# First layer's selective scan: softplus as one ScalarE function, one y image added to in all four directions, straight writes to PSUM

## The chip, the cores and the metric

The kernel runs on one core of one Trainium2 chip. A core has five engines with a queue each: TensorE (PE, matrix products, into PSUM), VectorE (DVE), ScalarE (ACT, functions from tables), GpSimd (POOL, no access to PSUM) and SyncE (SP, which here issues DMA transfers). They meet through semaphores alone. The metric is the device time of one launch in microseconds. A median of several runs is compared with a median; the profile is one further execution.

## What is computed

Two layers of a vision network, each a state-space (Mamba-like) mixer and a small quantised feed-forward net, on x of 4 x 48 x 64 x 64. The change touches the first mixer, after its convolution and projections:

```python
# z: 4 images x 96 channels x 64 x 64, K = 4 directions, one state per channel
x0 = z.reshape(B, D_INNER, L)                        # along rows
x1 = swapaxes(z, 2, 3).reshape(B, D_INNER, L)        # along columns
xs = stack([x0, x1, flip(x0), flip(x1)], axis=1)
x_dbl = einsum('bkdl,ked->bkel', xs, x_proj_weight)  # gives dts_r (3), Bs (1), Cs (1)
delta = softplus(einsum('bkrl,kdr->bkdl', dts_r, dt_projs_weight) + bias)
dA  = exp(delta * A)                                 # A = -exp(A_logs)
dBu = delta * Bs * xs
h[t] = dA[t] * h[t-1] + dBu[t]                       # scan over L = 4096 positions
y = h * Cs + Ds * xs
ym = y0 + unswap(y1) + flip(y2) + unswap(flip(y3))   # the four directions, in one image
```

Then come layer norm, an output product, and the rest of the network, which the change leaves alone.

## The kernel before

Five phases follow each other with a barrier between them: `front0_phase`, `scan0_phase`, `back0_phase`, `mid1_phase`, `back1_phase`. The change lies in `scan0_phase` (L821 to L1111).

**Tiling.** The 4 images x 32 channels of a group fill the 128 partitions, J = 3 groups (index j) cover the 96 channels. A direction's 4096 positions are walked in NTC = 4 pieces of TC = 1024. `steps` (L845) lists n = 16 steps for a group: directions 1 and 3 (down the columns, forward and back), then 0 and 2 (along the rows, forward and back), so 8 column steps and then 8 row steps; 48 steps in all. A half of a piece is CH = 512 positions, one bank of PSUM. i counts steps through all groups.

**A step, engine by engine.** TensorE makes dt before softplus in PSUM (`dt_of`, L925 to L936, tile q_dt, two halves, one buffer), and spreads B and C over the partitions half by half (`spread`, L938 to L945, tiles q_b and q_c, one buffer each). In a column step the moving operand is read in runs of 8 elements and the result is written with a stride through `by_rows`, so that PSUM holds the order of the scan. ScalarE computes |dt|, exp(-|dt|) and ln(1 + ..) (L991, L993, L995, tile b_l), VectorE adds max(dt, 0) to it (`delta_of`, L1014, tile b_dl): that is softplus. ScalarE makes the decay dA = exp(delta A) into PSUM (L983, tile b_qa). GpSimd multiplies delta by z (L1097, tile b_u; z is seen with a stride in a column step). VectorE multiplies that by B half by half (`drive`, L1020), scans (L1031, tile b_h) and multiplies by C (`times_c`).

**The sum over directions.** There are two images in SBUF, `yrow` and `ycol`. Direction 1 is written to `ycol` by `times_c` itself (L1044). The other three go through b_g (L1048) and are added by GpSimd (L1111) to `ycol` or `yrow`. ScalarE starts `yrow` as z times the sum of D (L1003). Before the last pieces GpSimd merges `ycol`, read with a stride, into `yrow` (`merge`, L1086, four times a group). SyncE stores the finished pieces.

**What sets the order.** It is written out by hand, in each engine's function. VectorE's turn for step i: first drive, first C product of step i-1, delta of i+1, second drive, second C product, scan. GpSimd: product of step i, then (from step 4 of a group) merge, then the add of step i-2. Buffers b_l, b_dl, b_u, b_h, b_g and b_qa are double.

## Time and profile before

| | us |
|---|---|
| median of 3 runs | 1626.08 |
| lowest, highest | 1622.43, 1626.56 |
| the profiled execution | 1625.65 |
| its span, first to last instruction | 1623.8 |
| first product of the scan on VectorE to the end of its last scan | 221.88 to 515.38 |

The page's groups name line, engine, output and inputs, shapes and count; then busy time and mean duration; then the idle time of the engine before such instructions and what ended it. The timeline gives start and duration; a bracket behind an instruction tells how long its engine idled and what released it, and its absence means that the engine was busy until then. Neighbouring instructions of an engine overlap by about 0.1 us, so cadence is read from starts.

### The profile page before, as it was taken

How to read it: one execution, taken by the hardware profiler on the slowest of the kernel's cores; microseconds unless marked ns; L12 is line 12 of the kernel's file. 1: busy time of each engine (PE TensorE's matmuls, PEld its weight loads, DVE VectorE, ACT ScalarE, POOL GpSimd, SP SyncE). 2: the span in 40 equal slices, each digit the busy share in tenths (PEclk: the TensorE clock that was granted, in tenths of full speed). 3: DMA queues.
4: the chain of work that ended last, by engine and by line, in shares of the span. 5: the costliest groups of instructions: out<-in, count | busy, mean ns of one | idle time of the engine just before them, and what ended most of it. 6: DMA issues, size and time to landing. Idle time of an engine off the chain costs nothing. (4 is left out here: it accounts for less than half of the span.)

```text
span 1623.8 us, 14529 instructions
## 1 busy us (share of the span) xinstructions
PE 1286.5 (79%) x3822; PEld 436.9 (27%) x3822; DVE 1271.7 (78%) x1274; ACT 1154.7 (71%) x1691; POOL 898.3 (55%) x451
## 2 busy tenths in 40 slices
PE   4999757585763577768789988998989889776995
PEld 2444201010110355532122222222222222111663
DVE  1665659999996477730999999999999999894775
ACT  2677358687773477748898898889898988641564
POOL 2400037969788333313987787888787888750000
PEclk8999955555555799978788889888897898555998
DMA  5344480200101233225877787777787877634572
GB/s 153 106 137 124 109 183 0 84 20 1 52 1 63 68 97 98 83 56 149 193 180 171 183 190 175 175 174 182 167 183 181 187 172 162 132 71 105 130 175 67
DMA packets 136429, 200.54 MB, mean 123 GB/s; under 512 B 26739, under 2 KB 68770, under 8 KB 135564
## 3 DMA queue, kind: packets, MB, share of 16 engines
q1 hardware_dynamic: 133740, 196.15, 49.5%
q10 hardware_dynamic: 2160, 2.61, 0.6%
q0 software_dynamic: 448, 0.85, 0.2%
q8 instruction: 32, 0.52, 0.1%
q14 instruction: 49, 0.40, 0.1%
HBM read 145.93 MB, written 53.63 MB: 123 GB/s over the span
## 5 line engine op out<-in xcount | busy, mean ns | idle before, releaser
L1375 POOL TENSOR_TENSOR m_ub<-m_dlb,m_bt 128x1536 f32<-128x1536 f32 x128 | 440.2, 3441 | 144.1 <-DVE m_h L1729 136.8
L1729 DVE TENSOR_TENSOR_SCAN m_h<-m_qa,m_state,m_ub 128x512 f32<-128x512 f32 x384 | 463.8, 1262 | 53.4 <-POOL m_ub L1375 51.9
L1691 ACT ACTIVATE m_qa<-m_dlb,k_a 128x512 f32<-128x512 f32 x384 | 254.8, 684 | 107.9 <-DVE m_h L1729 102.0
L1097 POOL TENSOR_TENSOR b_u<-b_dl,b_z 128x1024 f32<-128x1024 f32 x48 | 125.2, 2608 | 212.0 <-DVE b_dl L1014 211.4
L1740 DVE TENSOR_TENSOR m_g<-m_h,m_qc 128x1536 f32<-128x1536 f32 x128 | 221.7, 1732 | 14.3 <-issue 7.7
L1558 PE MATMUL m_qc<-m_bcr,k_selc 32*128 32x512 f32 x256 | 167.5, 738 | 81.8 <-DVE m_g L1740 81.6
L1575 PE MATMUL m_qy<-m_g,k_seld 128*32 128x512 f32 x768 | 169.5, 743 | 0.0
L944 PE MATMUL b_qb<-b_bc,k_pack_sel 96*128 96x512 bf16 x96 | 81.6, 850 | 73.6 <-DVE b_u L1020 71.0
L1499 PE MATMUL m_qf<-m_cva,k_conv 113*96 113x504 f32 (+1 forms) x192 | 124.4, 799 | 5.0 <-PEq L1131 5.0
L1558 PEld LDWEIGHTS m_qc<-m_bcr,k_selc 32*128 32x128 f32 x256 | 42.9, 209 | 205.7 <-issue 188.7
L983 ACT ACTIVATE b_qa<-b_dl,b_a 128x1024 f32<-128x1024 f32 x48 | 53.7, 1118 | 62.2 <-DVE b_dl L1014 62.2
L935 PE MATMUL b_qdt<-b_dt,b_wdt 75*128 75x512 bf16 x96 | 69.9, 852 | 34.0 <-DVE b_dl L1014 19.0
L526 PE MATMUL n_q<-a_cv,k_conv 113*96 113x504 f32 (+1 forms) x192 | 91.0, 611 | 2.6 <-DVE a_acc L545 2.4
L944 PE MATMUL b_qc<-b_bc,k_pack_sel 96*128 96x512 bf16 x96 | 84.1, 876 | 7.0 <-DVE b_g L1048 7.0
L1031 DVE TENSOR_TENSOR_SCAN b_h<-b_qa,b_h,b_u 128x1024 f32<-128x1024 f32 x36 | 84.5, 2347 | 0.0
L1020 DVE TENSOR_TENSOR b_u<-b_u,b_qb 128x512 f32<-128x512 f32 x96 | 65.0, 677 | 14.6 <-POOL b_u L1097 8.3
L1014 DVE SCALAR_TENSOR_TENSOR b_dl<-b_qdt,b_l 128x1024 f32<-128x1024 f32 x48 | 58.7, 1223 | 16.3 <-ACT b_l L995 16.1
L1499 PEld LDWEIGHTS m_qf<-m_cva,k_conv 113*96 113x96 f32 x192 | 41.1, 232 | 104.2 <-issue 104.2
L545 DVE SCALAR_TENSOR_TENSOR a_acc<-a_low,k_pack_d,n_q 96x512 f32<-96x512 f32 x32 | 23.7, 742 | 54.9 <-PE n_q L526 41.1
L991 ACT ACTIVATE b_l<-b_qdt 128x512 f32<-128x512 f32 x96 | 54.2, 590 | 13.9 <-PE b_qdt L935 12.7
L1657 ACT ACTIVATE m_tp<-m_u,k_pack_d 96x512 f32<-96x512 f32 x96 | 62.3, 712 | 0.8
L362 ACT ACTIVATE f_h<-g_q 96x1024 f16<-96x1024 f32 x32 | 32.6, 1020 | 39.0 <-PE g_q L356 39.0
(181 smaller groups left out, 2478.9 us busy)
## 6 DMA issues: line engine op xcount, KB each, us to landing
m_dlb<-scratch_dldu SPq DMA_DIRECT2D x128, 384.0 KB, 9.6
m_bt<-scratch_brow SPq DMA_DIRECT2D x128, 256.0 KB, 5.8
scratch_dldu<-m_dldu SPq DMA_DIRECT2D x32, 384.0 KB, 5.0
scratch_z<-a_z SPq DMA_DIRECT2D x24, 256.0 KB, 6.0
b_z<-scratch_z SPq DMA_DIRECT2D x3, 2048.0 KB, 11.4
scratch_y<-b_yrow SPq DMA_DIRECT2D x12, 512.0 KB, 2.6
c_y<-scratch_y SPq DMA_DIRECT2D x16, 384.0 KB, 3.4
scratch_gate<-m_gt SPq DMA_DIRECT2D x32, 192.0 KB, 4.8
```

What stands on the lines that cost most here:

```text
L526: last = self.nc.tensor.matmul(out[:, :, o], self.pairs[:, tap, :], src[:, :, i], start=(tap == 1), stop=(tap == 2))
L935: nc.tensor.matmul(by_rows(q_dt[:, v * CH:v * CH + CH], col), wdt[:, j, k, :], seen_rows(dtx[k][:], col, piece, v), start=True, stop=True) ...
L944: nc.tensor.matmul(by_rows(q[:], col), G["selbc0"][:, row + k, :], seen_rows(bcx[:], col, piece, v), start=True, stop=True).then_inc(ready, 1)
L1031: nc.vector.tensor_tensor_scan(h[s][:, way], q_a[s][:, way], u[s][:, way], carried, ALU.mult, ALU.add).then_inc(scanned, 1)
L1097: nc.gpsimd.tensor_tensor(by_column(u[s][:], col), by_column(dl[s][:], col), seen(z[j % 2][:], col, piece), ALU.mult).then_inc(u_ready, 1)
L1375: nc.gpsimd.tensor_tensor(ub[k % 3][:], dlb[u % 2][:, J:2 * J, :], bcast(bt[u % 2][:, n, :], J), ALU.mult).then_inc(ub_ready, 1)
L1499: nc.tensor.matmul(out[:, :, o], G["conv1"][:, tap, :], src[:, :, i], start=(tap == 1), stop=False)
L1558: nc.tensor.matmul(q_c[:], G["selc"][DI:P, 4 * n:4 * n + 4, :], bcr[u % 4][DI:P, :], start=True, stop=True).then_inc(c_mm, 1)
L1575: last = nc.tensor.matmul(q_y[32 * j:32 * j + 32, :], G["seld"][:], g[k % 2][:, j, :], start=(n == 0), stop=(n == 3))
L1691: nc.scalar.activation(q_a[:, j, :], dlb[u % 2][:, j, :], ACT.Exp, scale=G["a1"][:, j, n:n + 1]).then_inc(da, 1)
L1729: nc.vector.tensor_tensor_scan(h[k % 3][:, j, :], q_a[:, j, :], ub[k % 3][:, j, :], state[:, k % NS, j:j + 1], ALU.mult, ALU.add).then_inc ...
L1740: nc.vector.tensor_tensor(g[k % 2][:], h[k % 3][:], bcast(q_c[:], J), ALU.mult).then_inc(read, 1)
```

## The change

- Softplus is ScalarE's own function and reads q_dt: two halves a step, straight into b_dl. |dt|, Exp, Ln and VectorE's sum fall away. The function lies in another table than Exp, so steps are taken in pairs: load the Exp table, two decays (and perhaps a piece of y), load the softplus table, four softplus halves. b_dl has DL = 4 buffers.
- TensorE writes PSUM in the order in which it reads (`in_rows`). The readers of q_dt, q_b and q_c turn the order in a column step by their own pattern (`from_rows`, a step of 8 words).
- There is one y image, in the order of the rows, with two buffers b_y over the groups. Every direction goes through b_g, and GpSimd adds each piece to it; in a column step it reads and writes y with a stride. The merge falls away. y is begun for group 0 at the start and for the next groups in the last 8 steps of the one before.
- Direction 2 comes before direction 0, so that the last pass stores its pieces from 0 to 3.
- The loops run on over all 48 steps without a turn per group. TensorE's dt products for steps i+2 and i+3 stand in odd iterations, the first between the two halves of B and C.

The core of the diff:

```diff
-        yrow, ycol = (m.sb(f"b_{n}", [P, T]) for n in ("yrow", "ycol"))
+        y = [m.sb(f"b_y{r}", [P, T]) for r in range(2)]
...
+        dl = [m.sb(f"b_dl{s}", [P, TC]) for s in range(DL)]
...
-        order = [(1, 1, 0), (3, 1, 1), (0, 0, 0), (2, 0, 1)]
+        order = [(1, 1, 0), (3, 1, 1), (2, 0, 1), (0, 0, 0)]
...
-        def by_rows(ap, col):
+        def in_rows(ap, col):
-            return ap.rearrange("p (w h) -> p h w", h=H) if col else ap
+            return ap.rearrange("p (h w) -> p h w", h=H) if col else ap
+        def from_rows(ap, col):
+            return ap.rearrange("p (h w) -> p w h", h=H) if col else ap
...
# TensorE
-                pe.wait_ge(delta, freed(i, 1))
                 for v in range(TC // CH):
-                    nc.tensor.matmul(by_rows(q_dt[:, v * CH:v * CH + CH], col), wdt[:, j, k, :],
+                    pe.wait_ge(delta, half(i - 1, v))
+                    nc.tensor.matmul(in_rows(q_dt[:, v * CH:v * CH + CH], col), wdt[:, j, k, :],
...
+            for i in range(last + 1):
+                for o in range(2):
+                    if i < last:
+                        spread(i // n, i % n, o, q_b, 0, driven, b_mm)
+                    if i > 0:
+                        spread((i - 1) // n, (i - 1) % n, o, q_c, K4, read, c_mm)
+                    if o == 0 and i % 2 == 1:
+                        ahead(i, 2)
+                if i == 0:
+                    ahead(i, 2)
+                if i % 2 == 1:
+                    ahead(i, 3)
# ScalarE
-                            nc.scalar.activation(sp_l[s][:, part], q_dt[:, part], ACT.Abs).then_inc(absd, 1)
-                        nc.scalar.activation(sp_l[s][:], sp_l[s][:], ACT.Exp, scale=-1.0).then_inc(expd, 1)
-                        nc.scalar.activation(sp_l[s][:], sp_l[s][:], ACT.Ln, bias=G["eps"][:, 2:3]).then_inc(lnd, 1)
+            def delta_of(i):
+                s, col = i % DL, steps[i % n][1]
+                act.wait_ge(da_ready, freed(i, DL))
+                act.wait_ge(u_ready, freed(i, DL))
+                for v in range(TC // CH):
+                    part = slice(v * CH, v * CH + CH)
+                    act.wait_ge(dt_mm, half(i, v))
+                    nc.scalar.activation(by_column(dl[s][:, part], col), from_rows(q_dt[:, part], col), ACT.Softplus).then_inc(delta, 1)
...
+            for i in range(0, last, 2):
+                act.preload_act_table_set(LOG_EXP_SET)
+                decay(i)
+                decay(i + 1)
+                if i == 0:
+                    for c in range(NTC):
+                        begin_y(0, c)
+                if i // n + 1 < J and i % n >= n - 2 * NTC:
+                    begin_y(i // n + 1, (i % n - n + 2 * NTC) // 2)
+                if i + 2 < last:
+                    act.preload_act_table_set(SOFTPLUS_SET)
+                    delta_of(i + 2)
+                    delta_of(i + 3)
# VectorE
-                nc.vector.scalar_tensor_tensor(dl[s][:], q_dt[:], 0.0, sp_l[s][:], ALU.max, ALU.add).then_inc(delta, 1)
...
-                nc.vector.tensor_tensor(u[s][:, part], u[s][:, part], q_b[:], ALU.mult).then_inc(driven, 1)
+                half_u = by_column(u[s][:, part], col)
+                nc.vector.tensor_tensor(half_u, half_u, from_rows(q_b[:], col), ALU.mult).then_inc(driven, 1)
...
+                dve.wait_ge(added, freed(i))
+                nc.vector.tensor_tensor(by_column(g[s][:, part], col), by_column(h[s][:, part], col), from_rows(q_c[:], col),
+                                        ALU.mult).then_inc(read, 1)
# GpSimd
-                nc.gpsimd.tensor_tensor(part, part, ycol[:].rearrange("p (w h) -> p h w", w=W)[:, rows, :],
-                                        ALU.add).then_inc(merged, 1)
...
-                    nc.gpsimd.tensor_tensor(y, y, g[s][:], ALU.add).then_inc(added, 1)
+                    pool.wait_ge(added, done(i - 3))
+                    part = seen(y[j % 2][:], col, piece)
+                    nc.gpsimd.tensor_tensor(part, part, by_column(g[i % 2][:], col), ALU.add).then_inc(added, 1)
```

How the change moves the instructions is seen best in a row step in the middle of a pass. On VectorE, one row step before (b_u, b_qb: the drives; b_g, b_h, b_qc: the C products; the last line is the scan):

```order
L1020 TENSOR_TENSOR b_u1<-b_u1,b_qb 128x512
L1048 TENSOR_TENSOR b_g0<-b_h0,b_qc 128x512
L1014 SCALAR_TENSOR_TENSOR b_dl0<-b_qdt,b_l0 128x1024
L1020 TENSOR_TENSOR b_u1<-b_u1,b_qb 128x512
L1048 TENSOR_TENSOR b_g0<-b_h0,b_qc 128x512
L1031 SCALAR_TENSOR_TENSOR b_h1<-b_qa1,b_h0,b_u1 128x1024
```

And the same step in the changed kernel:

```order
L1021 TENSOR_TENSOR b_u1<-b_u1,b_qb 128x512
L1043 TENSOR_TENSOR b_g0<-b_h0,b_qc 128x512
L1021 TENSOR_TENSOR b_u1<-b_u1,b_qb 128x512
L1043 TENSOR_TENSOR b_g0<-b_h0,b_qc 128x512
L1032 SCALAR_TENSOR_TENSOR b_h1<-b_qa1,b_h0,b_u1 128x1024
```

The instruction that makes b_dl is gone, and only a C product is left between the two drives, each of which reads b_qb.

On ScalarE, one step of the second slice of a group before (b_l: the parts of softplus; b_qa: the decay; b_yrow: y begun):

```order
L983 ACTIVATE b_qa<-b_dl,b_a 128x1024
L991 ACTIVATE b_l<-b_qdt 128x512 x2
L993 ACTIVATE b_l<-b_l 128x1024
L995 ACTIVATE b_l<-b_l,k_pack_norm 128x1024
L1003 ACTIVATE b_yrow<-b_z,b_dsum 128x1024
```

And a pair of steps in the changed kernel:

```order
L999 ACT_TABLE_LOAD
L981 ACTIVATE b_qa<-b_dl,b_a 128x1024 x2
L990 ACTIVATE b_y<-b_z,b_dsum 128x1024
L1008 ACT_TABLE_LOAD
L974 ACTIVATE b_dl<-b_qdt 128x512 x4
```

Two steps' decays, then two steps' softplus, with a table load ahead of each kind.

On GpSimd, two row steps with a merge before (b_u: the product with z; the line that reads b_ycol: the merge):

```order
L1097 TENSOR_TENSOR b_u<-b_dl,b_z 128x1024
L1086 TENSOR_TENSOR b_yrow<-b_yrow,b_ycol 128x1024
L1111 TENSOR_TENSOR b_yrow<-b_yrow,b_g 128x1024
L1097 TENSOR_TENSOR b_u<-b_dl,b_z 128x1024
L1111 TENSOR_TENSOR b_yrow<-b_yrow,b_g 128x1024
```

And the column steps of the changed kernel, where the add has a form of 16 columns by 64 positions:

```order
L1074 TENSOR_TENSOR b_u<-b_dl,b_z 128x1024
L1085 TENSOR_TENSOR b_y<-b_y,b_g 128x16x64
L1074 TENSOR_TENSOR b_u<-b_dl,b_z 128x1024
L1085 TENSOR_TENSOR b_y<-b_y,b_g 128x16x64
L1074 TENSOR_TENSOR b_u<-b_dl,b_z 128x1024
```

Products and adds alternate in every step from the third on, and nothing stands between them.

## Rows read from the trace of the kernel before

**Rows 1.** The page: TensorE's busy us and share; granted clock in 40 slices.

```profile
PE 1286.5 (79%) x3822; PEld 436.9 (27%) x3822; DVE 1271.7 (78%) x1274; ACT 1154.7 (71%) x1691; POOL 898.3 (55%) x451
...
PEclk8999955555555799978788889888897898555998
```

**Rows 2.** Windows: length, busy us (count) by engine, granted clock, DMA share, GB/s.

```profile
250.00:283.00 33.00, 23.79 (x35) 3.28 (x33) 32.43 (x34) 26.70 (x30) 26.04 (x12) 0.50 0.00 0
450.00:483.00 33.00, 23.60 (x36) 3.55 (x36) 32.43 (x35) 26.50 (x31) 27.13 (x11) 0.50 0.00 1
```

**Rows 3.** Groups, 200 to 525 us: shapes, count, busy us, mean ns, idle before.

```profile
L1097 POOL TENSOR_TENSOR b_u<-b_dl,b_z 128x1024 f32<-128x1024 f32 x48 | 125.2, 2608 | 212.0 <-DVE b_dl L1014 211.4
...
L1014 DVE SCALAR_TENSOR_TENSOR b_dl<-b_qdt,b_l 128x1024 f32<-128x1024 f32 x48 | 58.7, 1223 | 16.3 <-ACT b_l L995 16.1
L1111 POOL TENSOR_TENSOR b_yrow<-b_yrow,b_g 128x1024 f32<-128x1024 f32 x24 | 56.5, 2353 | 1.1 <-POOL b_yrow L1111 0.2
...
L991 ACT ACTIVATE b_l<-b_qdt 128x512 f32<-128x512 f32 x96 | 54.2, 590 | 13.9 <-PE b_qdt L935 12.7
L983 ACT ACTIVATE b_qa<-b_dl,b_a 128x1024 f32<-128x1024 f32 x48 | 53.7, 1118 | 62.2 <-DVE b_dl L1014 62.2
...
L1086 POOL TENSOR_TENSOR b_yrow<-b_yrow,b_ycol 128x1024 f32<-128x1024 f32 x12 | 34.4, 2867 | 0.5 <-DVE b_g L1048 0.5
```

**Rows 4.** Timeline, row steps: start us, us, instruction [idle before <-releaser].

```profile
475.35 0.69 DVE L1020 TENSOR_TENSOR b_u<-b_u,b_qb 128x512 f32<-128x512 f32 x1
475.94 0.69 DVE L1048 TENSOR_TENSOR b_g<-b_h,b_qc 128x512 f32<-128x512 f32 x1
476.54 2.35 DVE L1031 TENSOR_TENSOR_SCAN b_h<-b_qa,b_h,b_u 128x1024 f32<-128x1024 f32 x1
...
477.83 2.87 POOL L1086 TENSOR_TENSOR b_yrow<-b_yrow,b_ycol 128x1024 f32<-128x1024 f32 x1
478.80 0.68 DVE L1020 TENSOR_TENSOR b_u<-b_u,b_qb 128x512 f32<-128x512 f32 x1
...
480.78 2.35 POOL L1111 TENSOR_TENSOR b_yrow<-b_yrow,b_g 128x1024 f32<-128x1024 f32 x1
...
483.10 2.35 POOL L1097 TENSOR_TENSOR b_u<-b_dl,b_z 128x1024 f32<-128x1024 f32 x1
...
485.47 0.69 DVE L1020 TENSOR_TENSOR b_u<-b_u,b_qb 128x512 f32<-128x512 f32 x1 [0.81 <-POOL b_u L1097]
```

**Rows 5.** Timeline, two column steps of the first slice.

```profile
254.33 1.12 ACT L983 ACTIVATE b_qa<-b_dl,b_a 128x1024 f32<-128x1024 f32 x1 [0.25 <-DVE b_dl L1014]
254.35 1.89 PE L935 MATMUL b_qdt<-b_dt,b_wdt 75*128 75x512 bf16 x2 [0.25 <-DVE b_dl L1014]
254.38 2.86 POOL L1097 TENSOR_TENSOR b_u<-b_dl,b_z 128x1024 f32<-128x1024 f32 x1 [3.25 <-DVE b_dl L1014]
...
258.38 1.03 PE L944 MATMUL b_qb<-b_bc,k_pack_sel 96*128 96x512 bf16 x1 [0.43 <-DVE b_u L1020]
...
260.44 1.12 ACT L983 ACTIVATE b_qa<-b_dl,b_a 128x1024 f32<-128x1024 f32 x1 [0.26 <-DVE b_dl L1014]
...
260.55 1.01 PE L935 MATMUL b_qdt<-b_dt,b_wdt 75*128 75x512 bf16 x2 [0.28 <-DVE b_dl L1014]
```

**Rows 6.** Timeline, the last steps, on VectorE, TensorE and GpSimd.

```profile
510.36 0.69 DVE L1020 TENSOR_TENSOR b_u<-b_u,b_qb 128x512 f32<-128x512 f32 x1 [0.81 <-POOL b_u L1097]
...
511.11 0.61 PE L944 MATMUL b_qb<-b_bc,k_pack_sel 96*128 96x512 bf16 x1 [3.15 <-DVE b_u L1020]
...
511.82 0.69 DVE L1020 TENSOR_TENSOR b_u<-b_u,b_qb 128x512 f32<-128x512 f32 x1 [0.18 <-PE b_qb L944]
...
513.03 2.35 DVE L1031 TENSOR_TENSOR_SCAN b_h<-b_qa,b_h,b_u 128x1024 f32<-128x1024 f32 x1
...
516.12 2.34 POOL L1111 TENSOR_TENSOR b_yrow<-b_yrow,b_g 128x1024 f32<-128x1024 f32 x1
...
516.85 0.69 DVE L1048 TENSOR_TENSOR b_g<-b_h,b_qc 128x512 f32<-128x512 f32 x1 [0.76 <-PE b_qc L944]
...
518.63 2.34 POOL L1111 TENSOR_TENSOR b_yrow<-b_yrow,b_g 128x1024 f32<-128x1024 f32 x1 [0.17 <-POOL b_yrow L1111]
```

**Rows 7.** Timeline, ScalarE in a later phase: a table load and softplus.

```profile
901.74 1.28 ACT L1674 ACT_TABLE_LOAD   x1
903.03 0.59 ACT L1678 ACTIVATE m_dldu<-m_qg 96x512 f32<-96x512 f32 x1
903.65 1.28 ACT L1679 ACT_TABLE_LOAD   x1
```

**Rows 8.** Timeline, the first steps of the scan.

```profile
220.73 1.03 PE L944 MATMUL b_qb<-b_bc,k_pack_sel 96*128 96x512 bf16 x1 [2.47 <-DMA b_bc<-scratch_bc]
221.88 0.69 DVE L1020 TENSOR_TENSOR b_u<-b_u,b_qb 128x512 f32<-128x512 f32 x1 [5.57 <-PE b_qb L944]
```

179 lines of the change are left out of this document (63 added, 116 removed).

## The prediction

> **What bounds the kernel now.** The change touches one phase, the first layer's scan, so I read that phase alone. The page shows a TensorE that runs at about half clock there: slices 5 to 12 of the clock line are 5s, and the windows say 0.50, the 1.2 GHz level [rows 1, 2]. The windows then name the engine: in 33 us VectorE is busy 32.43 us, ScalarE 26.6, GpSimd 26 to 27, TensorE under 24 [rows 2]. The scan's first product on VectorE starts at 221.88 [rows 8], its last scan instruction ends at 513.03 + 2.35 = 515.38 [rows 6]. That is 293.5 us for 48 steps, 6.11 a step. Three patterns make it up. (a) In a plain row step VectorE never rests: its scans stand 5.76 us apart, and the releasers are empty (476.54 to the next scan). (b) Where a merge falls, GpSimd runs four instructions for two steps' needs (product, merge 2.87, add 2.35, product 2.35), and VectorE waits 0.81 us for the product [rows 4]. (c) In a column step of the first slice the two decays lie 260.44 - 254.33 = 6.11 us apart: VectorE makes delta, TensorE needs 1.89 us for the next pair of dt products, ScalarE then does Abs, Exp and Ln, VectorE again [rows 5]. So three engines hold each other within 10%, and a cure for one shows only up to the next.
>
> **Rows, part by part.** Softplus moves to ScalarE, so VectorE's L1014 goes: 48 instructions of 1.22 us [rows 3], with a cadence of 1.13. What is left of a row step is pieced together from starts, since neighbours overlap by 0.1. Scan to the next drive: 478.80 - 476.54 = 2.26. Second drive to scan: 476.54 - 475.35 = 1.19 [rows 4]. First drive to second: the trace has one step without a delta instruction, the last one. There the second drive waits for TensorE (0.18 idle) and starts 511.82 - 510.36 = 1.46 after the first [rows 6]. Sum 2.26 + 1.46 + 1.21 = 4.93 us (the 1.21 is 513.03 - 511.82, from the same step). Of the 1.13 taken away, 0.28 comes back as a wait for q_b, which has one buffer.
>
> Is another engine later than 4.93? GpSimd has one product and one add, 2.35 each with starts 2.31 apart, 4.62; the merges (12 of 2.87 us) are gone [rows 3, 4]. ScalarE works in pairs of steps: two decays of 1.12, a table load, softplus in four halves, a table load. The trace has softplus and table loads in a later phase: a load takes 1.28, the next instruction starts 1.29 after it, and a 512-column softplus takes 0.59, the same as Abs today [rows 3, 7]. The second step's dt products may only start once the first half of q_dt has been read, about 0.75 later (start, 0.61, landing [rows 6]), so the four halves take 2.45 instead of 2.0. Pair: 2.2 + 1.3 + 2.45 + 1.3 = 7.25, with a begin_y of 1.13 it is 8.4, against 2 x 4.93 = 9.86. ScalarE has 1.5 us or more to spare, and the four delta buffers mean that its lateness in a pair is not handed to GpSimd. The dt products that now stand between two b products on TensorE wait for the first softplus half, 3.0 us after the scan before; TensorE is wanted there only at 4.9 + 0.7. So a row step costs 4.93, set by VectorE, and 24 of them 118.3 us.
>
> **Columns, part by part.** TensorE now writes PSUM straight and three readers hop instead. TensorE's own gain: a column product takes 1.03, a row product 0.61, a dt pair 1.89 against 1.01 [rows 5, 6]. I take 0.61, since the hop in PSUM goes away; the moving operand keeps its runs of 8, and if that was the cause it stays 1.03 (a rival below). The chain (c) is gone with Exp and Ln.
> The readers have no row in this trace. VectorE's four products per column step read q_b or q_c with a step of 8 words. Lower bound: no cost, nothing in the trace has VectorE slowed by a pattern; a gain is excluded, since no element is dropped. Upper bound from TensorE: hopping cost it (1.03 - 0.61)/512 = 0.82 ns a column, one more cycle of the granted 1.2 GHz. One more cycle for VectorE, whose own rate is (1.223 - 0.68)/512 = 1.06 ns a column [rows 3, 4], is 0.54 us a product. Between them stands GpSimd, which pays (2.86 - 2.35)/1024 = 0.50 ns an element for a hopping read of z [rows 3, 5], 0.26 us per 512. These two rows are equally near (one the same memory, the other a read), so I take their middle, 0.40 us a product. A step is then: first to second drive 1.19 + 0.8 = 1.99 (VectorE's own two products now outlast the wait for q_b, 1.46 + 0.40), second drive to scan 1.21 + 0.8 = 2.01, scan to drive 2.26: 6.26 us. At 0 it is 4.93, at 0.54 it is 6.82.
> GpSimd: the product stays 2.86 (2.82 between starts). The add now reads and writes y hopping. Lower bound 2.87, as the merge with one hopping operand; I take one further hopping stream at the same 0.51, 3.38; no row bounds a hopping write from above, and it would decide from 3.5 on. Step 2.82 + 3.34 = 6.16, just under VectorE's 6.26; with 2.87 it is 5.64. ScalarE with hopping reads of 0.4 more in four halves, 8.9 a pair, is far from 12.5. So 24 column steps take 24 x 6.26 = 150.2 us: hardly different from the 6.11 they take now, and the gain is all in the rows.
>
> The Trainium skill speaks against the column part. Its page "Vector Engine (DVE) Microarchitecture Reference", section 5.2, says that a VectorE stream keeps its full rate only in runs of two adjacent words, and gives 1.73 ns a column for one source that hops and 2.5 ns for small steps, both in SBUF. No run here shows it for PSUM. An estimate from that page's two figures, over its 1.05: 0.35 us a product would make the whole 1595, and 0.74 us would make it 1632.
>
> **The ends.** The first product waits for bc's load, not for delta: TensorE was released at 220.73 by the DMA [rows 8], so the start stays at 221.88. The four begin_y now stand early on ScalarE (4.5 us, behind decay 1), but delta of step 2 is wanted only once scan 0 is over, at about 226. At the end the two last adds run after each other, to 518.63 + 2.34 = 520.97; in the new order the second last is done before the last scan, and the last begins when its product ends, 516.85 + 0.69 = 517.54, plus 0.13. It ends at 520.0 where the scan ended at 515.38: 0.95 less [rows 6]. A second y tile frees the turn between groups of channels: nothing waits there now that a row shows, so zero.
>
> **Sum.** Steps: 150.2 + 118.3 = 268.5 against 293.5, 25.0 less; the end 0.95 less; later phases start earlier and are otherwise the same. The profiled execution took 1625.65 us (span 1623.8 and 1.85 around it), 0.4 below the median of the runs shown, 1626.08. 1625.65 - 25.9 = 1599.7, so **1600 us**.
>
> **Rivals.**
> (B) Hopping is free for VectorE and for GpSimd's write. Then GpSimd sets the column at 5.64, 24 x 5.64 = 135.4: 1585. For it: VectorE takes one element a cycle, and a memory word per cycle may be enough. Against it: both rows with hops show a price.
> (C) VectorE pays the whole extra cycle, 6.82 a step, 163.7 us: 1613.
> (D) Slower. The 8-word step costs VectorE more, say three cycles an element: 1.09 us more a product, 4.66 + 4 x 1.09 = 9.02 a step, 216.5 us: 1666. It decides from the point where the column step reaches (293.5 + 0.95 - 118.3)/24 = 7.3 us, 0.67 us more a product. The place is VectorE's L1021 and L1043 in column passes. Against it: both rows cost at most one cycle.
> (E) TensorE stays at 1.03 in columns, because its operand comes in short runs. b's product then delays the second drive to 1.88 + 0.40 = 2.28: 0.29 more, 24 times: 1607.
> (F) ScalarE becomes the bound of the rows. A switch would have to cost 2.66 instead of 1.30: pairs of 9.97, and of 11.1 in the two thirds of row steps that carry a begin_y, 16 x 5.55 + 8 x 4.99 = 128.7: 1610. The rows show 1.30 from instruction to instruction [rows 7]. It is the Trainium skill, page "ScalarE: Activation LUTs", section "What ACT_TABLE_LOAD costs", that gives 2.66 us with a drain; this trace does not agree.
>
> **How the numbers follow.** Forecast 0.30, B 0.22, C 0.24, E 0.08, F 0.03, D 0.07, others 0.06. The range from 1583 to 1617 takes in B and C, the bounds of the unknown costs, with 2 to 3 us for the phases behind, and holds above 8 in 10 of this. A measurement of this kernel tells 0.3% (5 us) from nothing. Faster by more: forecast, B, C, E, F, 0.87. Within: 0.05, part of the others and a mild D with 0.6 us a product. Slower: 0.08.
>
> **What would show it.** Row steps: scans 4.9 apart, a q_b wait of 0.2 before the second drive. Column steps: the duration of VectorE's 512-column product (0.68, 1.08 or 1.22) and of GpSimd's add in 16x64 form (2.87 or 3.4), and who releases the first drive: GpSimd means B, nobody means the forecast or C. TensorE's column product at 0.6. ScalarE with idle time before its decays, up to 5 us a pair. What would make it wrong: an add over 3.5 us, a product over 1.3, or table loads with gaps around them.

## The result, and the profile after

The changed kernel takes **1584.43 us** (median of 4 runs, 1573.58 to 1586.61) against 1625.76 for the kernel before (4 runs, 1622.43 to 1626.56): a ratio of 0.9736, 95% interval 0.9689 to 0.9783, or 41 us less where 26 were forecast. Measured again beside the experiments, the same program took 1580.31 us (ratio 0.9717, 0.9683 to 0.9752). Two of the experiments below were profiled in an execution with a lower granted clock (0.60 and 0.67); of those two traces only the scan is read, where the granted clock is the same 0.50 as in the others.

A block below is the 16 steps of one group of channels: 8 column steps, then 8 row steps. The page's engine line and clock line, to be held against [rows 1]:

```profile
PE 1235.0 (78%) x3822; PEld 436.1 (28%) x3822; DVE 1220.5 (77%) x1226; ACT 1110.7 (70%) x1643; POOL 905.2 (57%) x451
...
PEclk8999955555556999876988789887898978555997
```

VectorE lost 48 instructions and 51 us. TensorE lost 51 us with no instruction fewer. GpSimd has the same 451 instructions and 7 us more. The granted clock in the scan is again half of full speed (the 5s).

The windows (length, busy us and count of PE, PEld, DVE, ACT, POOL, clock, DMA share, GB/s), against [rows 2]:

```profile
260.00:300.00 40.00, 25.47 (x48) 5.00 (x48) 37.60 (x40) 29.77 (x34) 40.00 (x17) 0.50 0.03 6
...
390.00:440.00 50.00, 29.28 (x58) 5.89 (x58) 44.12 (x48) 33.30 (x39) 50.00 (x18) 0.50 0.05 21
...
227.12:467.90 240.78, 143.64 (x273) 28.39 (x273) 219.74 (x232) 165.78 (x188) 240.78 (x92) 0.50 0.12 39
```

The engine without idle time is no longer VectorE (32.43 of 33 before) but GpSimd: 40.00 of 40, 50.00 of 50, and 240.78 of 240.78 us over nearly the whole scan, row steps included. VectorE is busy 219.74 of these. The groups from 200 to 490 us, against [rows 3]; columns are count, busy us, mean ns, idle before and its releasers:

```profile
L1085 POOL TENSOR_TENSOR b_y<-b_y,b_g 128x1024 f32<-128x1024 f32 x48 | 129.7, 2703 | 3.9 <-DVE b_g L1043 3.9
L1074 POOL TENSOR_TENSOR b_u<-b_dl,b_z 128x1024 f32<-128x1024 f32 x48 | 124.4, 2594 | 155.9 <-DMA b_z<-scratch_z 151.5 <-DVE b_h L1032 4.4
...
L1021 DVE TENSOR_TENSOR b_u<-b_u,b_qb 128x512 f32<-128x512 f32 x96 | 65.3, 681 | 40.0 <-PE b_qb L939 27.2 <-POOL b_u L1074 12.8
L1043 DVE TENSOR_TENSOR b_g<-b_h,b_qc 128x512 f32<-128x512 f32 x96 | 65.2, 679 | 1.0 <-PE b_qc L939 0.8 <-issue 0.2
...
L939 PE MATMUL b_qb<-b_bc,k_pack_sel 96*128 96x512 bf16 x96 | 58.9, 613 | 100.7 <-DVE b_u L1021 92.4 <-DMA b_bc<-scratch_bc 8.1
L981 ACT ACTIVATE b_qa<-b_dl,b_a 128x1024 f32<-128x1024 f32 x48 | 53.6, 1118 | 57.7 <-DVE b_h L1032 57.5
L974 ACT ACTIVATE b_dl<-b_qdt 128x512 f32<-128x512 f32 x96 | 52.1, 594 | 20.7 <-PE b_qdt L930 19.9 <-POOL b_u L1074 0.6
...
L999 ACT ACT_TABLE_LOAD x24 | 30.8, 1283 | 0.4
```

Three readings. VectorE's 512-column products have a mean of 681 and 679 ns over rows and columns together, as long as a row product before [rows 4]: the hopping reads of PSUM cost nothing. GpSimd's two groups add up to 254.1 us. Before, its products, adds and merges took 125.2 + 56.5 + 34.4 [rows 3] and the 28.4 of one more group, the adds to `ycol`:

```profile
L1111 POOL TENSOR_TENSOR b_ycol<-b_ycol,b_g 128x1024 f32<-128x1024 f32 x12 | 28.4, 2364 | 0.0
```

That is 244.5 us, so it now does 10 us more work in a scan that is 44 us shorter. ScalarE waits 57.5 us for scans before its decays, so it has room.

Two column steps (start us, us, instruction, [idle before <-releaser]), to be held against [rows 5]:

```profile
238.11 0.69 DVE L1021 TENSOR_TENSOR b_u<-b_u,b_qb 128x512 f32<-128x512 f32 x1 [0.17 <-PE b_qb L939]
...
238.80 2.84 POOL L1074 TENSOR_TENSOR b_u<-b_dl,b_z 128x1024 f32<-128x1024 f32 x1
...
241.62 3.06 POOL L1085 TENSOR_TENSOR b_y<-b_y,b_g 128x1024 f32<-128x1024 f32 x1
241.68 0.69 DVE L1021 TENSOR_TENSOR b_u<-b_u,b_qb 128x512 f32<-128x512 f32 x1
...
244.34 2.28 DVE L1032 TENSOR_TENSOR_SCAN b_h<-b_qa,b_u 128x1024 f32<-128x1024 f32 x1
...
244.64 2.85 POOL L1074 TENSOR_TENSOR b_u<-b_dl,b_z 128x1024 f32<-128x1024 f32 x1
...
247.53 0.69 DVE L1021 TENSOR_TENSOR b_u<-b_u,b_qb 128x512 f32<-128x512 f32 x1 [0.90 <-POOL b_u L1074]
...
250.19 2.34 DVE L1032 TENSOR_TENSOR_SCAN b_h<-b_qa,b_h,b_u 128x1024 f32<-128x1024 f32 x1
```

GpSimd runs product, add, product without a gap: 2.82 + 3.02 = 5.84 us between the starts at 238.80 and 244.64. VectorE waits 0.90 us for its product, and the scans stand 250.19 - 244.34 = 5.85 apart. A row step, against [rows 4]:

```profile
277.84 2.34 DVE L1032 TENSOR_TENSOR_SCAN b_h<-b_qa,b_h,b_u 128x1024 f32<-128x1024 f32 x1
...
280.10 0.66 DVE L1021 TENSOR_TENSOR b_u<-b_u,b_qb 128x512 f32<-128x512 f32 x1
...
281.53 0.69 DVE L1021 TENSOR_TENSOR b_u<-b_u,b_qb 128x512 f32<-128x512 f32 x1 [0.17 <-PE b_qb L939]
...
282.74 2.34 DVE L1032 TENSOR_TENSOR_SCAN b_h<-b_qa,b_h,b_u 128x1024 f32<-128x1024 f32 x1
```

4.90 us from scan to scan, pieced together as forecast: 2.26, 1.43 with the wait for q_b, 1.21. Of the gain in the first block (98.9 us before from its first scan to the next block's, 82.5 now) 6.0 us lie in the first eight steps and 10.4 in the other eight.

All steps of the first block of 16, from scan to scan in us, read from the starts: columns 4.84, 4.90, 4.89, 5.03, 5.85, 5.87, 5.82, 5.31; rows 5.33, 5.32, 4.90, 4.89, 4.83, 4.90, 4.89, 4.89. The other two blocks differ at their start: their fourth step already takes 5.83 and 5.81, the third block's first 5.18. From the first product (222.49) to the end of the last scan (471.94) it is 249.45 us where it was 293.5; 268.5 was forecast. The end, against [rows 6]:

```profile
469.60 2.34 DVE L1032 TENSOR_TENSOR_SCAN b_h<-b_qa,b_h,b_u 128x1024 f32<-128x1024 f32 x1
...
474.19 2.34 POOL L1085 TENSOR_TENSOR b_y<-b_y,b_g 128x1024 f32<-128x1024 f32 x1 [2.09 <-DVE b_g L1043]
```

The last add ends 476.53 - 471.94 = 4.59 us after the last scan; it was 520.97 - 515.38 = 5.59.

By spans the trace lost 1623.8 - 1584.7 = 39.1 us: 44.05 in the scan, 1.0 at its end, less 0.6 for a later start and some 5 in the three phases behind it. Those 5 are no effect of the change: the phases behind the scan (from the first table load of the third phase to the end) take 1104.7 us in this trace, 1102.8 in the second trace of the same program, 1096.0 to 1102.8 in eight of the experiments, and 1099.4 before. They vary by 9 us between executions of code that none of these kernels touches.

### The profile page after: what moved, and what is told of

Same layout as the page of the kernel before. It is cut to its first block and busy times, and to the rows that moved or that the text cites. A ratio compares the mean times of both kernels' runs of the same rounds, so it can differ in the third digit from the quotient of the medians.

```text
span 1584.7 us, 14386 instructions
## 1 busy us (share of the span) xinstructions
PE 1235.0 (78%) x3822; PEld 436.1 (28%) x3822; DVE 1220.5 (77%) x1226; ACT 1110.7 (70%) x1643; POOL 905.2 (57%) x451
## 5 line engine op out<-in xcount | busy, mean ns | idle before, releaser
L1714 DVE TENSOR_TENSOR m_g<-m_h,m_qc 128x1536 f32<-128x1536 f32 x128 | 221.7, 1732 | 18.4 <-issue 12.5
L939 PE MATMUL b_qb<-b_bc,k_pack_sel 96*128 96x512 bf16 x96 | 58.9, 613 | 100.7 <-DVE b_u L1021 92.4
L1085 POOL TENSOR_TENSOR b_y<-b_y,b_g 128x1024 f32<-128x1024 f32 x48 | 129.7, 2703 | 3.9 <-DVE b_g L1043 3.9
L981 ACT ACTIVATE b_qa<-b_dl,b_a 128x1024 f32<-128x1024 f32 x48 | 53.6, 1118 | 57.7 <-DVE b_h L1032 57.5
L930 PE MATMUL b_qdt<-b_dt,b_wdt 75*128 75x512 bf16 x96 | 51.4, 625 | 21.2 <-DMA b_dt<-in_ones 14.9
L974 ACT ACTIVATE b_dl<-b_qdt 128x512 f32<-128x512 f32 x96 | 52.1, 594 | 20.7 <-PE b_qdt L930 19.9
L1043 DVE TENSOR_TENSOR b_g<-b_h,b_qc 128x512 f32<-128x512 f32 x96 | 65.2, 679 | 1.0 <-PE b_qc L939 0.8
L939 PE MATMUL b_qc<-b_bc,k_pack_sel 96*128 96x512 bf16 x96 | 58.9, 614 | 3.2 <-DVE b_g L1043 3.2
```

Source lines behind the costliest of these rows:

```text
L939: nc.tensor.matmul(in_rows(q[:], col), G["selbc0"][:, row + k, :], seen_rows(bcx[:], col, piece, v), start=True, stop=True).then_inc(ready, 1)
L1085: nc.gpsimd.tensor_tensor(part, part, by_column(g[i % 2][:], col), ALU.add).then_inc(added, 1)
L1714: nc.vector.tensor_tensor(g[k % 2][:], h[k % 3][:], bcast(q_c[:], J), ALU.mult).then_inc(read, 1)
```

## The experiments

In all of them the kernel before was run on the same chip beside them. "Scan" is the time from the first product on VectorE to the end of the last scan, from the trace.

| kernel | median us | ratio to before, 95% interval | scan us |
|---|---|---|---|
| before | 1625.6 to 1629.6 | 1 | 293.5 |
| changed kernel, measured again | 1580.31 | 0.9717 (0.9683 to 0.9752) | 249.8 |
| softplus from Abs, Exp, Ln and VectorE | 1608.87 | 0.9883 (0.9846 to 0.9919) | 277.5 |
| two images and merges | 1595.14 | 0.9809 (0.9788 to 0.9831) | 261.9 |
| TensorE writes with hops, readers straight | 1582.82 | 0.9728 (0.9700 to 0.9755) | 253.0 |
| GpSimd's add without hops | 1568.34 | 0.9624 (0.9592 to 0.9657) | 234.2 |
| VectorE's hop in SBUF, not PSUM | 1585.19 | 0.9742 (0.9720 to 0.9764) | 253.4 |
| one y tile | 1598.80 | 0.9825 (0.9806 to 0.9844) | 268.7 |
| ScalarE turns z | 1578.91 | 0.9704 (0.9683 to 0.9726) | 244.8 |
| the turn between the two decays | 1576.08 | 0.9699 (0.9676 to 0.9722) | 242.3 |
| table loads issued twice | 1581.03 | 0.9730 (0.9705 to 0.9754) | 249.7 |
| two more table loads a pair | 1599.93 | 0.9826 (0.9792 to 0.9859) | 268.4 |

**The changed kernel again.** 

> The changed kernel once more, word for word, for a second trace of it. The runs so far spread from 1573.6 to 1586.6. Theory: the scan's 48 steps take the same 249.5 us in this trace, and the spread is in a later phase with its granted clock. Rival: the spread comes from the scan's loads at its start or from GpSimd: the steps differ by several us.

1580.31 us, scan 249.78. The scan repeats within 0.4 us, the total within 4 us of medians. That the spread goes with the granted clock of a later phase is not shown. What is said of a step below rests on the scan, not on the total.

**Softplus undone.** With it go the table loads, the pairing of steps and TensorE's place for its dt products; the one image, its two buffers and the straight writes stay.

```diff
-                    nc.scalar.activation(by_column(dl[s][:, part], col), from_rows(q_dt[:, part], col), ACT.Softplus).then_inc(delta, 1)
+                    nc.scalar.activation(by_column(sp_l[s][:, part], col), from_rows(q_dt[:, part], col), ACT.Abs).then_inc(absd, 1)
+                nc.scalar.activation(sp_l[s][:], sp_l[s][:], ACT.Exp, scale=-1.0).then_inc(expd, 1)
+                nc.scalar.activation(sp_l[s][:], sp_l[s][:], ACT.Ln, bias=G["eps"][:, 2:3]).then_inc(lnd, 1)
...
+                    nc.vector.scalar_tensor_tensor(dl[s][:], q_dt[:], 0.0, sp_l[i % 2][:], ALU.max, ALU.add).then_inc(delta, 1)
```

> The changed kernel with softplus as before: Abs, Exp, Ln on ScalarE (one table, a step at a time), max and sum on VectorE (in a column step in two halves), TensorE's dt products at the end of each iteration; one y image, two y tiles and straight writes stay. Theory (VectorE reads PSUM with hops at no cost, so it is bound by its number of instructions): VectorE gets 1.13 us a step back, row steps 5.76, column steps about 5.85, 48 steps 279 us instead of the 249.5 us of the changed kernel, so about 1613. Rival (the one image without merges is what gave the time): row steps stay near 5.2, about 1595.

1608.87 us, 24 to 29 us over the changed kernel, scan 28.1 us longer. Its timeline, VectorE in a column step:

```profile
302.70 2.34 DVE L1039 TENSOR_TENSOR_SCAN b_h<-b_qa,b_h,b_u 128x1024 f32<-128x1024 f32 x1
...
306.14 1.27 DVE L1019 SCALAR_TENSOR_TENSOR b_dl<-b_qdt,b_l 128x512 f32<-128x512 f32 x2
...
308.53 2.34 DVE L1039 TENSOR_TENSOR_SCAN b_h<-b_qa,b_h,b_u 128x1024 f32<-128x1024 f32 x1
```

VectorE has no idle time in it and needs 5.83 us: the instruction that makes delta is back. All steps, rows and columns, stand 5.70 to 5.83 apart, but the first (7.70) and the last (4.88). So softplus is worth most of the gain, in rows and in the column steps that GpSimd doesn't hold.

**Two images and the merge back.** Softplus stays new.

```diff
+                    out = ycol[:, at:at + CH]
...
+                nc.gpsimd.tensor_tensor(part, part, ycol[:].rearrange("p (w h) -> p h w", w=W)[:, rows, :],
+                                        ALU.add).then_inc(merged, 1)
```

> The changed kernel with yrow, ycol and the four merges a group as before; softplus in one function and straight writes stay. Theory (GpSimd is the bound as soon as VectorE is relieved): two row steps cost GpSimd 4 x 2.31 + 2.85 = 12.1 us, 6.05 a row step against VectorE's 4.9; column steps fall to 4.9, since GpSimd has no adds in the first four and straight ones after; 24 x 6.05 + 24 x 4.95 = 264 us, 14 more than the changed kernel, about 1599. Rival (GpSimd's totals count, and they are lower here, 80 us a group against 84): 1580 or less.

1595.14 us, 11 to 15 us over the changed kernel, scan 12.5 us longer. Its timeline, row steps with a merge:

```profile
287.24 0.69 DVE L1023 TENSOR_TENSOR b_u<-b_u,b_qb 128x512 f32<-128x512 f32 x1 [2.31 <-POOL b_u L1093]
...
291.78 2.85 POOL L1081 TENSOR_TENSOR b_yrow<-b_yrow,b_ycol 128x1024 f32<-128x1024 f32 x1
```

Where merges fall VectorE waits 2.31 us and the step takes 7.25; at the start of the next block it is 8.04 and 8.37. GpSimd does less in all (in a block four adds fall away against four merges, and the other column adds are straight) and still costs more, since the work comes in lumps and the product's buffers only let it run a step ahead: in the early column steps it idles some 2 us before each product, until a scan or delta is done.

**TensorE writes PSUM with hops again**, and its readers read straight.

```diff
-            return ap.rearrange("p (h w) -> p h w", h=H) if col else ap
+            return ap.rearrange("p (w h) -> p h w", h=H) if col else ap
-            return ap.rearrange("p (h w) -> p w h", h=H) if col else ap
+            return ap.rearrange("p (w h) -> p h w", h=H) if col else ap
```

> The changed kernel with TensorE writing PSUM with hops in column steps as before and the readers straight. TensorE's column products go from 0.61 back to 1.03, VectorE's and ScalarE's durations do not move if hopping reads are free. Theory (columns are bound by GpSimd at 5.84, and VectorE's chain with the slow products is 5.56): only the column steps that GpSimd does not bind get longer, 0.3 to 0.6 us in 12 of them, 0 to 6 us in all, 1584 to 1591. Rival (the straight writes carried the column gain): all 24 column steps go to 6.1 or more, 1600.

1582.82 us: in the total no difference that can be measured, in the scan 3.2 to 3.6 us more. Its groups:

```profile
L939 PE MATMUL b_qc<-b_bc,k_pack_sel 96*128 96x512 bf16 x96 | 83.2, 867 | 4.4 <-DVE b_g L1043 4.4
L939 PE MATMUL b_qb<-b_bc,k_pack_sel 96*128 96x512 bf16 x96 | 80.7, 841 | 50.1 <-DVE b_u L1021 42.7 <-DMA b_bc<-scratch_bc 6.9
...
L1043 DVE TENSOR_TENSOR b_g<-b_h,b_qc 128x512 f32<-128x512 f32 x96 | 65.5, 682 | 5.3 <-PE b_qc L939 5.1
```

TensorE's products go from 614 to 867 ns in the mean, VectorE's stay at 682. In columns they take 1.03 to 1.14. The column steps then take 5.50 to 5.57 us, but the first and last of a block, set by the wait for q_b, where GpSimd would set some at 5.84 anyway. GpSimd's work for a block is 83.7 us in any case (worked out below), and the second block takes 84.1. TensorE's relief was real and was mostly covered by the next engine.

**GpSimd's add without hops** (it adds the columns in the order of the scan, so y holds other positions).

```diff
-                    part = seen(y[j % 2][:], col, piece)
-                    nc.gpsimd.tensor_tensor(part, part, by_column(g[i % 2][:], col), ALU.add).then_inc(added, 1)
+                    part = y[j % 2][:, piece * TC:piece * TC + TC]
+                    nc.gpsimd.tensor_tensor(part, part, g[i % 2][:], ALU.add).then_inc(added, 1)
```

> The changed kernel, but in column steps GpSimd adds b_g to y position by position, without turning the order; the two column directions are then left in column order in y, so what leaves the scan is another sum. All else stays. Theory (GpSimd, with 2.82 + 3.02 us a step, is the bound of the columns): its add falls from 3.06 to 2.35, its group of 16 steps from 84 to 78 us, and VectorE sets all steps at 4.9 to 5.1; 48 steps take about 238 instead of 249.5 us, the kernel about 1572. Rival (VectorE's wait for TensorE's q_b or ScalarE sets the columns): no change of the steps of 5.83, 1583.

1568.34 us, scan 234.24: all steps 4.83 to 4.93 us but one (5.17). Its groups and a column step:

```profile
L1085 POOL TENSOR_TENSOR b_y<-b_y,b_g 128x1024 f32<-128x1024 f32 x46 | 108.0, 2347 | 0.8 <-DVE b_g L1043 0.6
...
L1043 DVE TENSOR_TENSOR b_g<-b_h,b_qc 128x512 f32<-128x512 f32 x92 | 62.5, 679 | 0.3 <-issue 0.3
```

Shorter adds (2.35 instead of 3.06) take the waits away, and VectorE then runs the columns, hopping reads and all, at the rate of the rows. That shows two things at once: GpSimd was the bound of the columns, and PSUM's hops are free for VectorE. The 15 us between 249.5 and 234.2 are all that GpSimd costs. They follow from its sum over a block rather than from single steps, as is worked out in the section on the prediction.

**The hop in SBUF.** VectorE's C product reads h with the step of 8 words and q_c straight; it pairs values of other positions.

```diff
-                nc.vector.tensor_tensor(by_column(g[s][:, part], col), by_column(h[s][:, part], col), from_rows(q_c[:], col),
+                nc.vector.tensor_tensor(by_column(g[s][:, part], col), from_rows(h[s][:, part], col), by_column(q_c[:], col),
```

> The changed kernel, but in column steps the C product reads q_c straight and its SBUF operand h with the hops that q_c had (8 words); the order of the result is another, nothing is left out. Theory A (VectorE hops freely in either memory): L1043 stays at 0.68 us, no change, 1583. Theory B (free in PSUM alone; in SBUF a hop costs 0.35 us per 512, as the Trainium skill's page Vector Engine (DVE) Microarchitecture Reference, section 5.2, would have it): L1043 takes 1.03 us in columns and 0.68 in rows, mean 0.86; VectorE's column step becomes 5.4, still under GpSimd's 5.84, so 0 to 4 us more, up to 1587.

1585.19 us, scan 253.38. Its timeline, a column step:

```profile
243.90 2.34 DVE L1032 TENSOR_TENSOR_SCAN b_h<-b_qa,b_h,b_u 128x1024 f32<-128x1024 f32 x1
...
248.58 1.09 DVE L1043 TENSOR_TENSOR b_g<-b_h,b_qc 128x512 f32<-128x512 f32 x1 [0.17 <-issue]
249.59 2.28 DVE L1032 TENSOR_TENSOR_SCAN b_h<-b_qa,b_u 128x1024 f32<-128x1024 f32 x1
```

The same pattern that was free in PSUM takes a product from 0.68 to 1.09 us in SBUF: 0.41 us, 0.8 ns an element. All column steps go to 5.63 to 5.73 (one is 5.96), with VectorE as their bound. That is the price the forecast had put on PSUM (0.40), and here it gives a slower VectorE and no wait for GpSimd, as forecast. The step is longer than the sum of its parts: the forecast's chain with two slow products is 2.26 + 1.19 + 1.21 + 2 x 0.41 = 5.48, and the expectation said 5.4. Some 0.2 more come from a gap of 0.17 in front of the second C product, for which the trace names no releaser; TensorE's last q_c before it ended just then (248.49, start 247.88).

The Trainium skill, page "Vector Engine (DVE) Microarchitecture Reference", section 5.2, gives 1.73 ns a column where one source hops at every element, 0.68 over its 1.05 without, and 2.5 where both sources or the destination take small steps. The 0.8 of this run, with one source and a small step, lies between the two; for PSUM, of which the section's table doesn't speak, the traces show zero.

**One y tile.**

```diff
-            y = [m.sb(f"b_y{r}", [P, T]) for r in range(2)]
+            y = [m.sb("b_y", [P, T])] * 2
...
-                    if j >= 2:
-                        act.wait_ge(y_stored, 16 * NTC * (j - 1))
+                    if j >= 1:
+                        act.wait_ge(y_stored, 16 * NTC * j)
...
-                if i == 0:
+                if i % n == 0:
```

> The changed kernel with one y tile instead of two: y of a group is begun at the group's start, when the stores of the group before have landed. Theory as in the prediction (the second tile is worth nothing): 1583. Rival: ScalarE now waits at the group's first pair for the last add and its store (about 5 us after the scan before) and then makes four pieces (4.5 us), the softplus of the next steps comes late: 4 to 8 us at each of two group ends, 1591 to 1599.

1598.80 us, 14 to 19 us over the changed kernel. Two steps stand out, at the turns between blocks: 15.47 and 15.60 us instead of 4.84 and 5.18, more than the rival's 4 to 8 each. The scan is only 19.2 us longer, since GpSimd idles 9.5 us at the turn and so is not behind after it: in the second block the third and fourth step take 4.89 and 5.12 instead of 5.34 and 5.83. The timeline there:

```profile
313.30 4.26 ACT L990 ACTIVATE b_y<-b_z,b_dsum 128x1024 f32<-128x1024 f32 x4 [7.74 <-DMA scratch_y<-b_y]
...
319.52 1.10 PE L930 MATMUL b_qdt<-b_dt,b_wdt 75*128 75x512 bf16 x2 [11.88 <-ACT b_dl L974]
...
321.15 0.69 DVE L1019 TENSOR_TENSOR b_u<-b_u,b_qb 128x512 f32<-128x512 f32 x1 [10.80 <-PE b_qb L939]
```

ScalarE waits 7.74 us for the last store, and behind it in its queue stands the softplus for which TensorE and then VectorE wait. This is a cost of the one y image, which needs y begun from the first column piece on; the kernel before wrote direction 1 to `ycol` and began `yrow` in the second slice, and took 7.3 us at its turns.

**ScalarE turns z** for the second and third block, so that GpSimd reads it straight; y is begun in steps 4 and 6.

```diff
+            def turn_z(j, c):
+                act.wait_ge(u_ready, done(n * (j - 1) + 2 * NTC - 1))
+                act.wait_ge(z_loaded[j % 2], 16 * (j // 2) + 16)
+                nc.scalar.activation(by_column(zt[:, c * TC:c * TC + TC], 1), seen(z[j % 2][:], 1, c), ACT.Identity).then_inc(z_turned, 1)
...
-                    begin_y(i // n + 1, (i % n - n + 2 * NTC) // 2)
+                    turn_z(i // n + 1, (i % n - n + 2 * NTC) // 2)
```

> The changed kernel, with z of groups 1 and 2 copied by ScalarE into column order (four pieces a group, during the row steps of the group before), so that GpSimd's product reads straight in their column steps; y is begun two pieces at a time in steps 4 and 6. Theory (GpSimd is the bound of the columns, ScalarE has 1.5 us or more to spare in a pair): L1074 falls from 2.86 to 2.35 in 16 of 24 column steps, the steps of 5.83 become 5.33 in these groups; 2 x 3 to 4 us less, about 1576. Rival (ScalarE becomes late in the row pairs with 1.1 to 1.2 us more each): no gain or a loss, 1583 or more.

1578.91 us, scan 244.79. GpSimd's product falls to 2.35 in those columns and the waits for it vanish but for three of 0.3 to 0.4 us, but row steps with a turn take 5.37 to 5.41 and column steps with two beginnings of y 5.57. That is 4.7 us less in the scan, where the theory had 6 to 8. Its timeline there:

```profile
285.86 2.02 ACT L999 ACTIVATE b_zt<-b_z 128x1024 f32<-128x1024 f32 x1
...
289.84 1.10 PE L934 MATMUL b_qdt<-b_dt,b_wdt 75*128 75x512 bf16 x2 [1.83 <-ACT b_dl L978]
...
291.47 0.69 DVE L1033 TENSOR_TENSOR b_u<-b_u,b_qb 128x512 f32<-128x512 f32 x1 [0.75 <-PE b_qb L943]
```

The turn takes 2.02 us, the late softplus holds TensorE's dt product, that stands in front of the second B product, and VectorE waits 0.75 instead of 0.17.

**The turn between the two decays**, where ScalarE waited 1.03 us for a scan.

```diff
                 decay(i)
+                if i // n + 1 < J and i % n in (4, 6):
+                    for c in range(2):
+                        begin_y(i // n + 1, i % n - 4 + c)
+                if i // n + 1 < J and i % n >= n - 2 * NTC:
+                    turn_z(i // n + 1, (i % n - n + 2 * NTC) // 2)
                 decay(i + 1)
```

> Edit: as in the run in which ScalarE turns z for blocks 1 and 2 and begins y early, but the turns and the two beginnings of y stand between the two exponentials of a pair of steps, no longer behind the second. In that run's trace a turn took 2.01 us, and the pairs of row steps that hold one took 5.41 + 4.89 us, because TensorE's product of dt, which waits for the softplus, came late and stood in front of the second product of B (VectorE waited 0.75 us for it). ScalarE meanwhile waited 1.03 us for the scan in front of its second exponential. My theory: put into that wait, the turn delays softplus by about 1.0 us and not by 2.0, as little as the beginning of y (1.13 us) did in the changed kernel, whose row pairs with it took 4.83 + 4.90; so eight row pairs lose 0.5 us each and the four pairs of column steps with two beginnings (5.57 + 4.89) 0.7 each at most: scan stage 244.8 to about 239 to 241 us, the run about 5 us under the 1578.9 of that kernel, 1572 to 1576, ratio about 0.967. Rival: the first exponential of the pair is the late one, the gap before the second is an artefact of that, and nothing changes: 244.8, 1579.

1576.08 us, scan 242.26: every row step with a turn is back at 4.84 to 4.90, and the columns of the second block run at 4.89 up to the sixth step. The 2.5 us gained are less than the 4 to 6 expected: the last steps of the columns and first of the rows (5.24, 5.36, 5.33, 5.34) are set by GpSimd again. Its work in a block with turned z is 8 x (2.31 + 3.02) + 8 x 4.62 = 79.6 us, and the second block takes 79.9, of which GpSimd is busy 79.7. In the run before, the block took 81.6 with GpSimd busy 79.9 of them: there ScalarE's delays came first. This kernel's median is 4 to 8 us under those of the changed kernel, and its ratio (0.9676 to 0.9722) touches the changed kernel's two intervals; in the scan the 7 us are plain.

**Every table load issued twice.** 

> Edit: the changed kernel with every table load of the stage's loop issued twice, 94 loads where it has 47. A load took 1.28 us and ScalarE waits 1.3 to 2.2 us for a scan in every pair of steps. My theory: ScalarE is off the path with a slack of about 1.5 us a pair in front of softplus (a beginning of y of 1.13 us in a pair of row steps costs nothing in the trace, a turn of z of 2.01 costs 0.52). A second load delays softplus by 1.28 us: nothing in pairs without the beginning of y, about 0.9 us in the four row pairs a block that hold one, in blocks 0 and 1; scan stage 249.5 plus 4 to 8 us, 253 to 258, the run 1586 to 1592. Rival: ScalarE is on the path and each load costs its full time, 47 x 1.28 = 60 us, 1640. Second rival: the chip skips a load of the table that is already there, which the trace would show as a short load, and the time stays at 1580 to 1584.

1581.03 us, scan 249.70. The trace holds the same 24 and 23 loads as without the edit: the second load of a table that is already there leaves no record and costs nothing (the second rival, but for the short load it expected). Whether the chip skips it or it never reaches the chip is not shown. So this run says nothing about ScalarE's slack; it is one more measurement of the changed kernel.

**Two more loads in front of each pair's softplus**, with a change of table.

```diff
                     act.preload_act_table_set(SOFTPLUS_SET)
+                    act.preload_act_table_set(LOG_EXP_SET)
+                    act.preload_act_table_set(SOFTPLUS_SET)
```

> Edit: in front of each pair's softplus the changed kernel loads the softplus table once; here it loads softplus, exp, softplus: two loads more a pair, 46 more in all (a second load of the table already there left no record in the run before this one, so it takes a change of table to cost anything). Each pair's softplus comes 2.57 us later. My theory: the slack in front of softplus is about 1.5 us in a pair of row steps (1.13 us of a beginning of y cost nothing, 2.01 us of a turn of z cost 0.52), and a late softplus is paid through TensorE, whose product of dt waits for it in front of the second product of B. So about 1.1 us for each of the 4 row pairs of block 2 and the early column pairs of every block, about 2.2 us for the 8 row pairs with a beginning of y, nothing in the column steps that GpSimd holds at 5.84: in all some 20 to 28 us, scan stage 270 to 277, the run 1602 to 1610. Rival: no slack, each load paid in full, 46 x 1.28 = 59 us, 1640. Second rival: more slack than I think, since two of the four softplus are needed only a step later: under 8 us, 1581 to 1589.

1599.93 us, scan 268.44. A pair of steps becomes 6.03 + 4.90 us where it was 2 x 4.9, and 7.10 + 4.90 where it holds a beginning of y: 1.13 and 2.2 us more, as reckoned. The sum is 19 us, just under the 20 to 28 expected, since the columns that GpSimd held at 5.84 turn into 6.03 + 4.90 and so give some back. Its groups and timeline:

```profile
L999 ACT ACT_TABLE_LOAD x24 | 30.8, 1283 | 0.4
...
298.14 0.69 DVE L1023 TENSOR_TENSOR b_u<-b_u,b_qb 128x512 f32<-128x512 f32 x1 [2.44 <-PE b_qb L939]
```

2.57 us of delay cost 1.13 in a plain pair: ScalarE's slack in front of softplus is 1.4 us a pair. The kernel as changed uses 1.13 of it for the beginning of y, at no cost.

## Why the prediction was right in its direction and 16 us short

The range, 1583 to 1617, holds the measured 1584.43 by 1.4 us; the second median, 1580.31, lies under it. That the first fell inside is luck.

**Row steps: right.** 4.93 forecast, 4.83 to 4.90 measured in the steps that VectorE sets. The part that came back as a wait for q_b was 0.17 instead of 0.28. The first two or three row steps of a block take 5.32, which the forecast had not: they pay for the columns.

**TensorE's column product: right.** 0.61 where it was 1.03. It was the hopping write that cost, not the operand's short runs; rival E (1607) falls with it. The run with hopping writes brings 1.03 and more back, and shows how little it is worth: 3.2 to 3.6 us.

**VectorE's hop: the step that failed.** The forecast took 0.40 us a product, the middle between GpSimd's price for a hop in SBUF (0.26) and one more cycle an element, reckoned from TensorE's hopping write (0.54). It is 0 in PSUM, for VectorE and for ScalarE (median of softplus 592 ns in column steps, 597 in row steps). With it VectorE's column step fell from 6.26 to 4.9, under GpSimd's, and rival B's mechanism, GpSimd as the column bound, came true. The run with the hop in SBUF shows that the price itself was sound for the other memory (0.41); the forecast's chain from it to the step was 0.2 short there (5.48 against 5.63 to 5.73).

**GpSimd's add: mis-sized.** 3.38 forecast, 3.06 measured (3.02 between starts): the hopping write costs 0.20 us over the one hopping read, not 0.51. That makes the column step 2.82 + 3.02 = 5.84.

**The slower engine of each step, step by step: the second failed step.** The forecast charged every column step and every row step with the engine that is slower in it. Only three or four of the eight column steps in a block take GpSimd's 5.84. GpSimd's product for step i may run once scan i-2 is over, so GpSimd can be up to 4.9 - 2.82 = 2.1 us ahead of VectorE's need; a column step uses that up, and a row step, in which GpSimd needs 4.62 of 4.9, gives 0.28 back. Where it never gets back to the full 2.1, its sum counts. From the product of step 2 (227.12) to the end of the add of step 45 (467.90) GpSimd has no idle time: 46 products and 46 adds, 22 x 2.82 + 24 x 2.31 + 24 x 3.02 + 22 x 2.31 = 240.8 us, and the window has 240.78. A whole block is 8 x 5.84 + 8 x 4.62 = 83.7 us of GpSimd's time, against 78.1 of VectorE's (a block in the run with straight adds); the second block takes 390.86 - 307.14 = 83.72, between these two scans:

```profile
307.14 2.28 DVE L1032 TENSOR_TENSOR_SCAN b_h<-b_qa,b_u 128x1024 f32<-128x1024 f32 x1
...
390.86 2.28 DVE L1032 TENSOR_TENSOR_SCAN b_h<-b_qa,b_u 128x1024 f32<-128x1024 f32 x1
```

The first takes 82.46, since no adds of an earlier block stand beside its first two products and its reserve is full.

Where VectorE feels it follows from the order. An add follows its product by two steps. So there are three intervals with a row product beside a column add, 2.31 + 3.02 = 5.33; the trace has 5.31, 5.33, 5.32. From the steps alone the row steps of 4.9 look like VectorE's own, but GpSimd is catching up in them. By this reckoning a quicker VectorE there would bring nothing but longer waits in the columns; no run has tried that. Three others bear the reckoning out. With turned z GpSimd's sum is 79.6 and the block takes 79.9. With straight adds it is 78.0, and the block takes VectorE's 78.1, with no wait for GpSimd. And where VectorE's columns are slowed to 5.7 (the hop in SBUF), a block takes 84.5, hardly more than 83.7.

The forecast's 6.26 and 4.93 made 268.5 us, 19 more than the 249.45 of the trace. About 10 of these are the price of the hops (24 x 0.42 down to 5.84), about 7.5 the step-by-step reckoning (8 x 5.84 + 8 x 4.93 = 86.2 a block, where the sum gives 83.7), and the rest is the start, where GpSimd has its reserve. Rival B, with 5.64 for all 24 columns and a sum of 253.7, was near by two errors that partly cancel: an add 0.2 too cheap, and the same reckoning step by step.

**The ends: right**, 1.0 us against 0.95. The start came 0.6 us later: TensorE was released by the load of B and C at 221.77 instead of 220.73, and its shorter product gave 0.4 of that back.

**The second y tile: zero against the kernel before, but not a part without worth.** Without it the changed kernel takes 10.6 and 10.4 us more at its two turns. The forecast named no cost for beginning y a block ahead, and did not say that the second tile is what pays for it.

**ScalarE and the table loads: right.** 1.28 us a load, 0.4 us of idle time in front of 24 of them, slack 1.4 us a pair; the forecast had said 1.5 for a pair with a beginning of y, where 0.3 is left. It counted that slack against the length of a pair of steps, while what decides is when TensorE's dt product, in front of the second B product, gets its half. The rival with dear table switches is excluded. The figure of 2.66 us a switch in the Trainium skill, page "ScalarE: Activation LUTs", section "What ACT_TABLE_LOAD costs", is not what these traces show: two more loads a pair delayed it by what 2 x 1.28 explains.

**Parts alone.** Measured by taking each out of the changed kernel: softplus 24 to 29 us, one image instead of two with merges 11 to 15, straight writes 3 in the scan and nothing measurable in the total. The sum is near the 41 to 47 us that the change brings, though they need not add up. The new order of the directions and the loops without a turn were not taken out alone.

## What to carry to other kernels

A stride has a price for each pair of engine and memory, and a price from another pair is not an estimate of it: where the range hangs on it, forecast with both ends and look which engine is next, since that engine caps the loss. Where two engines meet through small buffers and each is the slower one in some steps of a cycle, compare their sums over the cycle, not the slower of each step: the buffers' slack is given once, at the start, and an engine without idle time over many steps is the bound even where the cadence is another's. Work that arrives in lumps on a side engine can cost more than a larger amount spread evenly.
